# Five expert tiles moved into the last chain block of a linear-attention and mixture-of-experts kernel

## What is computed

```python
def step(S, inp):
    k_t, q_t, v_t, beta_t, a_t = inp
    S = S * a_t[..., None, None]
    kv_mem = jnp.einsum('bhd,bhde->bhe', k_t, S)
    delta = (v_t - kv_mem) * beta_t
    S = S + k_t[..., :, None] * delta[..., None, :]
    y_t = jnp.einsum('bhd,bhde->bhe', q_t, S)
    return (S, y_t)
...
ctx = _rmsnorm(ys, norm_w) * jax.nn.silu(gate)
x = _layernorm(x + ctx @ Wo.T + bo)
...
routing_indices = jnp.argmax(router_logits, axis=-1)
for e in range(8):
    xe = jnp.where(routing_indices == e, x, 0.0)
    ye = (silu(xe @ gate_w[e].T) * (xe @ up_w[e].T)) @ down_w[e].T   # 128 -> 352 -> 128
    out = out + jnp.where(routing_indices == e, ye, 0.0)
x = _layernorm(x + out)
```

## Time and profile before

| | us |
|---|---|
| median of 3 runs (770.83 to 773.49) | 773.37 |
| time of the profiled execution | 774.71 |
| its span on the core | 772.9 |
| PE busy | 651.5 (84%) |
| DVE busy | 632.9 (82%) |
| POOL busy | 601.4 (78%) |
| ACT busy | 416.5 (54%) |

### The profile page before, as it was taken

One profiled execution on the slowest core, in us unless ns is written; L12 is line 12 of the kernel. 1 busy time (PEld: TensorE's weight loads), 2 busy tenths in 40 slices (PEclk: granted clock), 3 DMA queues, 4 the chain that ended last, 5 costly groups with the idle time before them and its releaser, 6 DMA issues.

```text
span 772.9 us, 13851 instructions
## 1 busy us (share of the span) xinstructions
PE 651.5 (84%) x3513; PEld 499.5 (65%) x3513; DVE 632.9 (82%) x1701; ACT 416.5 (54%) x1313; POOL 601.4 (78%) x758
## 2 busy tenths in 40 slices
PE   8668698889989887897988999496879979999990
PEld 3435374747657464664747556384778979999990
DVE  3899999999999999999999999999892535666530
ACT  6736456565565665566566546432324446666651
POOL 2888787979999899999999999999561527444574
PEclk9989799899999999999999999789669999999996
DMA  6734243341625334262433515304534655776730
GB/s 175 199 100 99 47 121 84 85 124 51 157 60 131 96 91 106 73 157 70 126 93 89 122 51 136 88 22 159 195 106 138 205 215 175 254 245 232 233 118 9
DMA packets 135919, 97.28 MB, mean 126 GB/s; under 512 B 95630, under 2 KB 110225, under 8 KB 135714
## 3 DMA queue, kind: packets, MB, share of 16 engines
q1 hardware_dynamic: 130514, 87.55, 40.2%
q0 software_dynamic: 4320, 8.43, 3.3%
q10 hardware_dynamic: 1008, 0.43, 0.2%
HBM read 39.80 MB, written 31.43 MB: 92 GB/s over the span
## 4 chain that ended last, share of the span: by engine, by line
PE 33%; DVE 31%; POOL 19%; issue 7%; ACT 6%; DMA 2%; ACTq 0%; DVEq 0%; POOLq 0%; SPq 0%
PE banks L436 12%; DVE banks L1904 6%; PE banks L449 6%; DVE banks L1878 5%; POOL q_prod L1311 5%; DVE upd L1892 5%; DVE prod L1862 4%; DVE banks L1888 3%; DVE mix L1882 3%; PE banks L695 3%; POOL u L1311 3%; DVE upd L1873 3%; PE banks L849 2%; PE banks L676 1%; POOL kkqk L1311 1%
## 5 line engine op out<-in xcount | busy, mean ns | idle before, releaser
L1311 POOL TENSOR_TENSOR q_prod<-s_keep,q_gam 128x512 f32<-128x512 f32 x128 | 140.5, 1099 | 15.8 <-ACT d_keep L1012 8.6
L1008 ACT ACTIVATE s_keep<-banks 128x128 f32<-128x128 f32 x128 | 50.2, 392 | 179.2 <-DVE upd L1892 177.2
L752 PE MATMUL banks<-q_prod,ident 128*128 128x240 f32 (+1 forms) x496 | 112.6, 381 | 24.6 <-POOL q_prod L1311 24.6
L752 PEld LDWEIGHTS banks<-q_prod,ident 128*128 128x128 f32 x496 | 93.9, 194 | 44.9 <-POOL q_prod L1311 35.0
L1904 DVE TENSOR_REDUCE banks<-upd 128x128 f32<-128x640 f32 x128 | 105.8, 826 | 7.7 <-DVE upd L1892 0.5
L436 PE MATMUL banks<-xs_t,w_tile 128*128 128x128 f32 x852 | 108.9, 278 | 3.6 <-issue 2.7
L545 POOL DMA_INDIRECT out<-rows_out,xs x71 | 70.0, 986 | 51.5 <-ACT rows_out L526 43.4
L436 PEld LDWEIGHTS banks<-xs_t,w_tile 128*128 128x128 f32 x852 | 102.3, 194 | 4.8 <-issue 4.4
L580 DVE TENSOR_TENSOR hid<-banks,silu 128x384 f32<-128x384 f32 x71 | 39.6, 557 | 72.9 <-PE banks L436 42.2
L1878 DVE TENSOR_REDUCE banks<-prod 128x64 f32<-128x576 f32 x128 | 93.6, 732 | 0.0
L1862 DVE TENSOR_TENSOR prod<-banks,k_gam 128x512 f32<-128x512 f32 x128 | 88.3, 690 | 3.4
(11 more groups left out here) (224 smaller groups left out, 1454.9 us busy)
## 6 DMA issues: line engine op xcount, KB each, us to landing
w_tile<-gate_up_we SPq DMA_DIRECT2D x71, 352.0 KB, 3.1
xs<-x_sorted SPq DMA_DIRECT2D x71, 64.5 KB, 2.2
x_ct<-in_x_ct SPq DMA_DIRECT2D x16, 256.0 KB, 3.0
k_dram<-kq_s SPq DMA_DIRECT2D x16, 256.0 KB, 2.9
q_dram<-kq_s SPq DMA_DIRECT2D x16, 256.0 KB, 3.9
out<-v_s SPq DMA_DIRECT2D x16, 256.0 KB, 2.6
out<-beta SPq DMA_DIRECT2D x16, 256.0 KB, 3.4
k_h<-k_dram SPq DMA_DIRECT2D x16, 256.0 KB, 3.2
```

The source lines that it names most:

```text
L752: i = mm(out, ident[:, :], q_prod[m][:, d, :, 1 - m:], start=(m == 0 and d == 0), stop=(d == DH - 1), skip_group_check=True)
L1311: b.step(label, win, lambda: tt(out, x, y, op))
```

## The change

The numbers of tiles that are worked on before the loop proper go up from 6 to 12 steps on PE and DVE. Two tiles go through gate and up beside the chain, and DVE multiplies them in three pieces each in the `between` places of chunks 4, 5 and 7; the third is placed before `y1_6`, the fourth and fifth before and behind `y1_7`. The weights of gate and up are loaded at block 14 and those of down at block 4. ACT takes the mean out of down_we, in 24 pairs of small instructions in blocks 6 to 13, where DVE did it in three large ones. `table_a` goes from chunks 5 to 7 of block 15 to blocks 13 and 14. POOL sorts the last three groups of the first 9 windows ahead of its ctx in block 15. Window 14's output side uses the same PSUM bank as all others (so its residual product waits for the logits of window 13), its layer norm root is taken on POOL, and its scaled copy (`x1`) comes in block 16. The group of tiles whose roots POOL takes at once has 17 instead of 13, they are normed two for each step from step 18 on, behind the step's other ACT work, and SP's fill rows come after the weights of tile 21.

```diff
-        NR, NX, NV, NG, NH, NO = 32, 4, 24, 6, 3, 12
-        KEPT = 17
-        PE_TAIL, ACT_TAIL, DVE_TAIL = 6, 4, 6
-        FILL_AT, AHEAD = 13, 4
+        NR, NX, NV, NG, NH, NO = 32, 4, 24, 6, 4, 12
+        KEPT, EARLY = 21, 5
+        PE_TAIL, ACT_TAIL, DVE_TAIL = 12, 10, 12
+        FILL_AT, AHEAD = 22, 4
...
         def turn_ps(tile):
+            if tile < EARLY:
+                return pb[5][:, IC * P:]
             return pb[0] if tile < TA or tile % 2 == 0 else pb[7]
...
+        def expert_turn(eng, tile):
...
+                if tile < EARLY:
+                    after(eng, s_silu, tile - 2)
+                nc.tensor.transpose(turn_ps(tile)[:, 0:P], xs[tile % NR][:, 0:D], ident[:, :]).then_inc(s_xturn, 1)
...
-                after(eng, s_xt, tile)
+                after(eng, s_xt, tile + 1 if tile + 1 < EARLY else tile)
...
-                return step - 6
+                return min(step - 6, 2 * (step - NORM + 1))
...
-                if step == NORM:
-                    for tile in range(normed(step)):
-                        norm(tile)
                 expert_act(eng, step)
-                if step > NORM:
-                    for tile in range(normed(step - 1), normed(step)):
-                        norm(tile)
+                for tile in range(normed(step - 1), normed(step)):
...
+        def expert_hid(eng, tile, first=0, last=IC):
+            if 0 <= tile < NF:
+                if first == 0:
+                    after(eng, s_silu, tile)
+                    after(eng, s_up, tile)
+                    after(eng, s_down, tile - NH)
+                at = slice(first * P, last * P)
+                ins = nc.vector.tensor_tensor(hid[tile % NH][:, at], u_ps(tile)[:, at], silu[tile % 2][:, at], ALU.mult)
+                if last == IC:
+                    ins.then_inc(s_hid, 1)
...
+        CENTRE = 6
...
-                if win < NW - 2:
-                    b.wait(act, "logits", win - 1)
-                    b.wait(dve, "ends", min(win - 1, NW - 5))
-                if win == NW - 2:
-                    b.wait(act, "kq_s", NW - 1)
-                    b.wait(dve, "before", NW - 4)
-                    b.wait(dve, "ends", NW - 4)
-                if win == NW - 1:
-                    b.wait(act, "logits", NW - 3)
-                    b.wait(act, "y_r0", win)
+                b.wait(act, "logits", win - 1)
+                b.wait(dve, "ends", min(win - 1, NW - 5))
...
                 y_sums(p, pre_ps[:, 2, 0:2 * T])
+                if not b.dry:
+                    expert_turn(b.eng, 0)
                 turn(o)
-                b.wait(act, "kq_s", NW - 1)
-                b.wait(act, "y_r0", p - 1)
+                if not b.dry:
+                    expert_pe(b.eng, -2)
+                b.wait(act, "y_r0", p)
                 count(w - 3)
...
+                if not b.dry:
+                    expert_pe(b.eng, -1)
                 attention(p)
                 late_chunks("y1", 4, 6)
+                if not b.dry:
+                    expert_turn(b.eng, 3)
+                    expert_gate_up(b.eng, 2)
                 late_chunks("y1_6", 6, 7)
                 return
             if b.tail:
+                if not b.dry:
+                    expert_turn(b.eng, 4)
+                    expert_gate_up(b.eng, 3)
                 b.wait(dve, "y_next", p)
                 late_chunks("y1_7", 7, 8)
+                b.wait(act, "d_keep7", p)
+                if not b.dry:
+                    expert_turn(b.eng, 5)
+                    expert_gate_up(b.eng, 4)
                 b.wait(dve, "y_prod2", p)
                 y_deltas()
+                if not b.dry:
+                    expert_down(b.eng, 0)
+                    expert_down(b.eng, 1)
...
+            def centre_down(j):
+                n = 3 * (w - CENTRE) + j
+                if not 0 <= n < IC * E:
+                    return
+                block = down_we[:, :, :, :].rearrange("p c e d -> p (c e) d")[:, n, :]
+                if n == 0:
+                    b.wait_dma(s_wdown, 1)
+                b.step(f"mean{n}", w, lambda: A(down_sc[:, :], block, ACT.Copy, scale=-1.0 / D, accum_out=down_neg[:, n:n + 1]))
+                b.wait(act, f"mean{n}", w)
+                b.step(f"centred{n}", w, lambda: A(block, block, ACT.Identity, bias=down_neg[:, n:n + 1]))
...
+                if not b.dry:
+                    nc.scalar.preload_act_table_set("silu_and_others")
+                    expert_turned(b.eng, 0)
                 x1_turned(o)
                 keep(NCH * w + 3)
-                router_logits(o)
+                if not b.dry:
+                    expert_turned(b.eng, 1)
+                    expert_silu(b.eng, 0)
                 keep(NCH * w + 4)
                 fill(4 * w + 3)
+                router_logits(o)
                 keep(NCH * w + 5)
-                variance(p)
-                log_root(p)
-                x1(p)
+                if not b.dry:
+                    expert_turned(b.eng, 2)
+                    expert_silu(b.eng, 1)
                 keep(NCH * w + 6)
                 keep(NCH * w + 7)
+                variance(p)
+                squared_root(p)
+                if not b.dry:
+                    expert_turned(b.eng, 3)
+                    expert_silu(b.eng, 2)
                 return
             if b.tail:
+                if not b.dry:
+                    expert_turned(b.eng, 4)
+                    expert_silu(b.eng, 3)
+                x1(o)
+                if not b.dry:
+                    expert_turned(b.eng, 5)
+                    expert_silu(b.eng, 4)
                 y_square()
+                if not b.dry:
+                    nc.scalar.preload_act_table_set("natural_log_exp_and_others")
                 x1_turned(o)
...
                 y_lags()
+                sort_to(w0, WA * TW)
                 context(o)
                 q_times_s(w, 0)
-                sort_to(w0, w0 + 2)
                 q_times_s(w, 1)
-                sort_to(w0 + 2, w0 + 4)
+                sort_to(WA * TW, w0 + 4)
                 q_times_s(w, 2)
...
+                places = ((0, 3), (1, 0), (1, 1), (1, 2), (2, 1), (2, 2), (3, 3), (3, 4))
+                if w in (NW - 3, NW - 2) and (c, k) in places:
+                    table_a_part(len(places) * (w - NW + 3) + places.index((c, k)))
...
-                if c == 3 and k < 3:
-                    route_part(r, 5 + k)
                 if c == 3 and 3 <= k:
                     if k == 3:
                         b.wait(act, "y_r1", p)
                     y_n_part(k - 3)
                 if c == 4 and k < 3:
                     y_n_part(2 + 2 * k, 2)
-                if c == 4 and k == 4:
+                if c == 5 and k < 3:
+                    route_part(r, 5 + k)
+                if c == 6 and k == 4:
                     route_part(r, 8)
-                if c == 5 and k == 0:
+                if c == 7 and k == 0:
                     route_part(r, 9)
-                if c == 5 and 1 <= k:
-                    table_a_part(k - 1)
-                if c == 6:
-                    table_a_part(4 + k)
-                if c == 7 and k < 2:
-                    table_a_part(9 + k)
+                if c == 0 and k == 3:
+                    pad_weights()
+                for n, parts in enumerate((((4, 4), (5, 3), (5, 4)), ((7, 2), (7, 3), (7, 4)))):
+                    if (c, k) in parts and not b.dry:
+                        expert_hid(b.eng, n, parts.index((c, k)), parts.index((c, k)) + 1)
+            def pad_weights():
+                if not b.dry:
+                    for n in range(NG):
+                        nc.vector.memset(w_tile[n][:, 2 * I:I + IC * P], 0.0).then_inc(s_wpad, 1)
...
-                    for k in range(n_table_a, n_steps_a):
-                        table_a(e, k)
-                    centre_down(e)
+                    expert_hid(e, 2)
+                    expert_hid(e, 3)
+                    expert_hid(e, 4)
+                    expert_sum(e, 0)
+                    expert_sum(e, 1)
...
-                e.wait_ge(s_sorted_a, 16 * WA * TW)
                 for tile in range(NG // 2):
                     load_weights(e, tile)
-                    load_rows(e, tile)
-                for tile in range(NG // 2, NG):
+                e.wait_ge(s_sorted_a, 16 * WA * TW)
+                for tile in range(NG):
                     load_rows(e, tile)
                 y_store()
                 load_weights(e, NG // 2)
-                load_rows(e, NG)
-                load_rows(e, NG + 1)
                 y_load()
+                b.wait(pe, "res", p)
+                e.dma_start(x_res[:, :], t["x_ct"][:, w, :]).then_inc(s_xres, 16)
                 for tile in range(NG // 2 + 1, NG):
                     load_weights(e, tile)
-                for tile in range(NG + 2, KEPT):
+                for tile in range(NG, 2 * NG):
                     load_rows(e, tile)
-                for tile in range(NG, FILL_AT - 2):
```

(14 more changed lines are left out.)

247 lines of the change are left out of this document (127 added, 120 removed).

## The result

The changed kernel takes 767.59 us in the median of 12 runs (764.3 to 771.29), the kernel before 773.43 beside it (770.33 to 774.61): a ratio of 0.9934, 95% interval [0.9913, 0.9954]. It is faster by 0.7%, 5.8 us; the forecast was 17.4 us. The forecast value, 756, lies far outside what was measured, and the median is 2.6 us above the range of 750 to 765. The profiled execution took 767.66 us, with a span of 765.8.

What follows compares the result with a forecast made beforehand. DVE's chain bounds until 568 us, then PE at 2.13 us a tile. Tile 70 at 733.5 plus a 21.4 tail gives a 754.9 span, 755.4 beside the median, stated as 756; own range 751 to 760, 8 in 10 750 to 765.

Steps and rivals of the forecast that it cites:

- The step that failed: Table steps moved from chunks 5 to 7 into blocks 13 and 14: 0.8 us out, 0.8 in, zero.
- blocks 6 to 13 longer than 33.5 us each: Listed sign, in the blocks with the centring pairs, that would show the forecast wrong.
- rival C: Slower: centring on ACT delays `keep` in blocks 6 to 13, up to 24 us, giving 780; chance 0.04.
- The centring at zero: 24 ACT pairs in blocks 6 to 13, 1.0 us each, covered by 3.05 us idle ahead of `keep`: priced 0.
- The end of the chain: DVE's last state in block 15: -2.1 + 0.7 + 0.6 + 0.2 = -0.6 us, so at 567.8.
- The stall of 2.09: DVE's wait for PE's count, now read in chunk 5 instead of 3: goes, 2.1 us less.
- rival A: PE holds the chain; hid pieces in chunk 7 wait, chain and sums 4 to 6 us later: 761; chance 0.17.
- the six pieces and the memsets: In the chain on DVE: six hid pieces cost 0.6 us (bound 1.7), six memsets 0.2.
- From the chain to the sums: PE behind; y1_6 at about 571.3, full clock from 560, sums of squares end at 583.8, 2.2 us later.
- The loop: From 583.8: 138.5 us of tiles plus 8.2 of narrow work, half of 6.0 us kept; tile 70 at 733.5.
- The stalls at tiles 13 and 17: PE's loop waits: 2.72 us and slow clock (about 1.5) go; of 2.7 about 0.3 is left.
- rival B: Loop waits move and stay: row loads before tile 9's weights, 17 roots block ACT; +10, 766; chance 0.12.

Runs made afterwards that it cites:

- run 1: Changed kernel with table_a's small values in PSUM bank 0 and its 16 steps at new places; ratio to the kernel before 0.9968.
- run 2: Changed kernel with only the new places of the 16 table steps, data left in SBUF; ratio to the kernel before 1.0019.
- run 7: run 6 plus the PSUM values and places of run 1, and one input of the table's last step in PSUM; ratio to the kernel before 0.9898.
- run 5: Changed kernel with the eight y_n parts back in the places of the kernel before; ratio to the kernel before 1.0006.
- run 4: Changed kernel without the centring of down_we (24 ACT pairs left out); ratio to the kernel before 1.0016.
- run 6: run 5 plus q_squares back in front of keep 0 and a block's first centring pair behind the square of y; ratio to the kernel before 0.9989.

## Why the prediction was wrong

**The step that failed** is this one: "The table steps leave chunks 5 to 7 and come into blocks 13 and 14: same DVE instructions, about 0.8 us out and 0.8 in, zero." They are not the same. The diff moves their data from PSUM to a new SBUF tile, and blocks 13 and 14 are full of POOL work; of the 6.2 us, 1.2 are the steps and 5.0 the memory they use (runs 1, 2, 7; 4.1 to 7.0 if any of the eight traces is put in place of the first). The Trainium skill states the rule, on its page "SBUF — State Buffer", section "SBUF: two separate sides": VectorE in a two-port mode, or with two SBUF inputs beside a GpSimd instruction that reads SBUF, and GpSimd lock one pair of ports in turn, and the other one blocks for the whole instruction. The traces agree (1.45 us instead of 0.15), and go beyond it: the last step in run 1 lost to three POOL instructions in a row, not one. The rule would have pointed at these steps, though not at the price: seven of the 16 have two inputs in the new SBUF tile or its like, and six more copy, shift or scale from SBUF to SBUF, which can be read from the kernel. None of the chain's own large steps has two SBUF inputs: each product reads one operand from PSUM, and the reductions have one input.

**A step that wasn't there.** The prediction prices the moved DMAs and the centring, but not y_n's later places, which it doesn't mention: a term left at nothing without a reason. They cost 2.8 us over nine blocks (run 5), by way of SP's queue, k's round trip through DRAM, and POOL, which has little idle time: in the kernel before it waited only 0.2 to 0.6 us for k_h in most blocks of 33.5 us. Its sign, "blocks 6 to 13 longer than 33.5 us each", was on the list and did show in six of the eight; its cause was not rival C.

**The centring at zero:** held (run 5, where it stayed and blocks 4 to 12 took 301.70 us, before 301.88; run 4).

**The end of the chain:** forecast 0.6 us less for block 15, measured 1.5. The stall of 2.09 went in full, y_next waits 0.39, and chunk 7 did idle for 0.70, so a part of rival A came true. That leaves 0.5 us less for what was put in and taken out: the eleven table steps that left the chain are worth at most the 1.2 us of all sixteen (run 7), so the six pieces and the memsets cost 0.7 at most, forecast 0.8.

**From the chain to the sums:** counted from the start of block 15 the last sums end at 50.0 us (forecast 52.0). y1_6 started at 580.29, forecast 571.3 + 10.7 = 582.0, where 10.7 is the late start of the block. The clock was 0.74 in 560 to 580 and 1.00 from 580; with the same shift the forecast had full speed from 570.7, and gate and up of tile 1 did run at 1.60 us from 574.09, where tile 0 had taken 2.93.

**The loop:** 745.03 - 592.50 = 152.5 us, forecast 149.7. The stalls at tiles 13 and 17 are gone as predicted. The 2.33 at tile 9, which rival B named with its cause, and the lower clock behind it (1.7) are more than the difference; the rest came out 1.2 us better than forecast. B's other waits didn't come: PE has no other over 0.3 us from 593 us on.

**The tail:** 20.8 against 21.4.

In sum: +10.7 in front of block 15, -2.0 from its start to the last sums of squares, +2.8 in the loop, -0.6 at the end, 10.9 in all; 754.9 + 10.9 = 765.8, the span. From the start of block 15 on the forecast is right to 0.2 us, and part of that is luck, since -2.0, +2.8 and -0.6 cancel. I had looked only there. With the two steps and the order of the weights mended the kernel takes 754.5; that this is near 756 is luck as well, since the forecast kernel didn't have the new order, worth 4.3 us. And the measured 767.6 is near rival B's 766, but of B's mechanism only the wait at tile 9 came.

## What to carry to other kernels

When an instruction is moved, compare its operands too: on VectorE two inputs in SBUF, or a copy from SBUF to SBUF, beside a busy GpSimd can cost ten times the instruction's own time (1.45 us instead of 0.15), and it shows as a duration, not as a wait. Small scalars of a side computation belong in PSUM if the main chain can't afford a stall.

A part that moves by about a microsecond (1.2 us here) in front of a queue that works in order moves all that is behind it; follow it to the engine with the least slack, even if that engine isn't touched.

Measure a gain on more than one chip when it rests on a stage that another chip runs differently.

## What the runs showed of the hardware that was not expected

- A VectorE step of eight elements with both inputs in SBUF took 2.42 us beside POOL, through the ends of two POOL instructions without getting in between, and ended with the third (run 1). The reductions with one SBUF input were held in no run (0.37 to 0.38 us). Copies of 8 and of 29 elements were (1.45 in the first trace, 0.94 in run 2), and so was the one-input shift on int32, where POOL started beside it. It took 0.15 us in the first trace and 1.13 in run 6:

```profile
473.42 1.13 DVE L278 TENSOR_SCALAR tab<-tiles_i 1x8 int32<-1x8 int32 x1
473.43 1.10 POOL L1380 TENSOR_TENSOR q_prod<-s_keep,q_gam 128x512 f32<-128x512 f32 x1
```

- The same program took 773 us on some chips and 788 to 790 on others, 2% apart. In the traces the difference lies in the expert loop, in gaps of 3.2 to 6.5 us between tiles that are 2.12 apart elsewhere. The traces with these gaps are those that lack half of the landing records, and the cause is open.
